# Layer 0 projection of a two-layer transformer: the bias rows in single-pass matmuls over 33 rows

## The reference, cut to what matters

```python
q = (layernorm(x, ln_q_g, ln_q_b) @ Wq + bq)            # 256 -> 256
kv = (layernorm(x, ln_kv_g, ln_kv_b) @ Wkv + bkv)       # 256 -> 512
q = apply_rotary(q * scale, x); k = apply_rotary(k * scale, x)
qn = layernorm(q, ln_h_g, ln_h_b); kn = layernorm(k, ln_h_g, ln_h_b)
```

## Time and profile before

| what | us |
|---|---|
| median of three runs | 2167.97 |
| the profiled execution, whole | 2167.56 |
| its span | 2165.9 |
| weights block, to the start of the next | 0 to 24.9 |
| projection block | 24.9 to 181 |
| PE busy in the span | 1929.3 (89%) |
| DVE busy in the span | 1472.4 (68%) |

### The profile page before, as it was taken

The page is one execution under the profiler, slowest core; times in us unless marked ns, Lnnn a source line. Parts: engine busy times, 40 slices in busy tenths (PEclk is TensorE's granted clock), DMA queues, the critical chain, the costliest instruction groups (busy, mean ns, idle before and its releaser), DMA issues. The chain is left out here.

```text
span 2165.9 us, 40750 instructions
## 1 busy us (share of the span) xinstructions
PE 1929.3 (89%) x11376; PEld 1297.2 (60%) x11438; DVE 1472.4 (68%) x3391; ACT 1222.2 (56%) x2508; POOL 896.3 (41%) x905
## 2 busy tenths in 40 slices
PE   4997999999959759999739899999998999999998
PEld 1452333333237659999725477777754777777787
DVE  4896888888548859999539576677365565653442
ACT  0683777777735237777314467767344777773331
POOL 1341000000027757798244187887300666662300
PEclk7895999999979979999969899999998999999999
DMA  7963000000072258899522011211101011111000
GB/s 205 289 145 59 2 0 0 1 0 1 1 203 96 98 172 265 265 282 279 178 66 61 4 47 42 57 45 49 35 1 39 24 25 35 25 35 39 11 10 20
DMA packets 185944, 173.87 MB, mean 80 GB/s; under 512 B 19651, under 2 KB 170741, under 8 KB 184822
## 3 DMA queue, kind: packets, MB, share of 16 engines
q1 hardware_dynamic: 173750, 143.23, 23.9%
q0 software_dynamic: 10720, 29.44, 4.1%
q10 hardware_dynamic: 1376, 0.02, 0.0%
HBM read 96.15 MB, written 61.60 MB: 73 GB/s over the span
## 5 line engine op out<-in xcount | busy, mean ns | idle before, releaser
L2633 POOL TENSOR_TENSOR w_rest<-work,w_head 128x512 fp32r<-128x512 f32 (+3 forms) x384 | 395.4, 1044 | 212.6 <-ACT w_head L2598 205.1
L767 DVE TENSOR_REDUCE half_max<-m_ps 128x1 f32<-128x512 f32 x512 | 317.4, 684 | 58.1 <-PE m_ps L689 57.7
L824 ACT ACTIVATE weights<-s_ps 128x512 f32<-128x512 f32 x512 | 266.2, 600 | 108.1 <-PE s_ps L707 108.1
L2594 ACT ACTIVATE work<-s_ps 128x512 f32<-128x512 f32 (+3 forms) x384 | 187.5, 488 | 113.2 <-PE s_ps L2423 91.1
L2598 ACT ACTIVATE w_head<-work 128x512 fp32r<-128x512 f32 (+3 forms) x384 | 201.4, 524 | 72.9 <-PE o_ps L2433 65.8
L689 PE MATMUL m_ps<-kT,qT 96*128 (+1 forms) x512 | 204.3, 400 | 8.4 <-DVE half_max L767 6.4
L707 PE MATMUL s_ps<-qT,kT 99*128 (+1 forms) x512 | 193.3, 384 | 9.5 <-DMA qT<-max_rows 5.1
L2433 PE MATMUL o_ps<-w_head,lat_head 128*128 128x512 f32 (+3 forms) x384 | 177.9, 463 | 7.1 <-POOL w_rest L2633 7.1
L864 POOL COPY v_now<-v 128x83 f32 (+1 forms) x64 | 16.0, 256 | 366.6 <-PE o_ps L719 361.7
L2474 DVE CUSTOM_DVE_ANT_0 work<-m_ps,mask_row 128x128 bf16<-128x128 f32 (+3 forms) x256 | 120.3, 485 | 49.2 <-PE m_ps L2391 46.2
L1072 POOL TENSOR_TENSOR gv_rest<-ex_wgv,gv_head 128x736 fp32r<-128x736 f32 x64 | 114.3, 1786 | 69.4 <-ACT gv_head L1169 69.4
(11 more groups left out here) (404 smaller groups left out, 5044.3 us busy)
## 6 DMA issues: line engine op xcount, KB each, us to landing
slots<-zero SPq DMA_DIRECT2D x8, 3456.0 KB, 27.5
rows<-slots SPq DMA_DIRECT2D x64, 256.0 KB, 3.4
slots<-ex_out SPq DMA_DIRECT2D x64, 256.0 KB, 3.0
ex_wgv<-in_L_ffn_wg_dram SPq DMA_DIRECT2D x72, 176.0 KB, 3.0
ex_wgv<-in_L_ffn_wv_dram SPq DMA_DIRECT2D x72, 176.0 KB, 3.3
ex_wo<-in_L_ffn_wo_dram SPq DMA_DIRECT2D x72, 128.0 KB, 3.2
oT<-work SPq DMA_DIRECT2D x64, 128.0 KB
w_down<-l_inverse SPq DMA_DIRECT2D x32, 256.0 KB, 3.9
```

The lines of the kernel that those rows point to most:

```text
L767: dve.tensor_reduce(half_max[:, u:u + 1], m_ps[:, BANK[u], :], AX.X, ALU.max).then_inc(max_done, 1)
L824: act.activation(w[:, s % 2 * 4 + j, :], s_ps[:, BANK[4 * s + j], :], ACT.Exp, scale=HD ** -0.5).then_inc(w_done, 1)
L2594: act.activation(w[:, s % 3, c0:512], s_ps[:, s % 3, c0:512], ACT.Exp, scale=SM1).then_inc(d["w_done"], 1)
L2633: pool.tensor_tensor(w_rest[:, s % 3, c0:512], w[:, s % 3, c0:512], w_head[:, s % 3, c0:512], ALU.subtract).then_inc(d["w_rest_done"], 1)
```

## The change

The bias row is split into a head, rounded to fp32r, and the remainder. Both stand in `bias_qkv`, now 33 partitions of fp32r: the head in row 0, the remainder in row 32, zeros between. The stationary operand is a block of ones of 33 partitions by 128 in fp32r. The bias matmul contracts 33 rows, once. POOL makes the zeros and ones in the weights block; the fp32 row of ones and its memset in `constants` go. DVE writes the sum to `bias_in`, copies it to row 0 and subtracts into row 32.

```diff
-        bias_qkv = l.sb("bias_qkv", [1, 3 * D])
+        bias_qkv = l.sb("bias_qkv", [BIAS_REST + 1, 3 * D], F32R)      # BIAS_REST = 32
+        ones = l.sb("bias_ones", [BIAS_REST + 1, P], F32R)
...
-            dve.memset(c.ones_row[:, :], 1.0)
...
-            dve.tensor_tensor(bias_qkv[0:1, 0:512], bias_ps[0:1, 0, :], bias_in[0:1, 0:512], ALU.add)
-            dve.tensor_tensor(bias_qkv[0:1, 512:768], bias_ps[0:1, 1, 0:256], bias_in[0:1, 512:768], ALU.add)
+            dve.tensor_tensor(bias_in[0:1, 0:512], bias_ps[0:1, 0, :], bias_in[0:1, 0:512], ALU.add).then_inc(summed, 1)
+            dve.tensor_tensor(bias_in[0:1, 512:768], bias_ps[0:1, 1, 0:256], bias_in[0:1, 512:768], ALU.add
+                              ).then_inc(summed, 1)
+            dve.wait_ge(summed, 2)
+            dve.wait_ge(blank, 4)
+            dve.tensor_copy(bias_qkv[0:1, :], bias_in[0:1, :]).then_inc(split, 1)
+            dve.wait_ge(split, 1)
+            dve.tensor_tensor(bias_qkv[BIAS_REST:BIAS_REST + 1, :], bias_in[0:1, :], bias_qkv[0:1, :], ALU.subtract)
+        @block.gpsimd
+        def _(pool):
+            pool.memset(plain[:, 0:3 * D], 0.0).then_inc(blank, 1)
+            pool.memset(plain[:, 3 * D:], 1.0).then_inc(blank, 1)
+            pool.wait_ge(blank, 2)
+            pool.tensor_copy(bias_qkv[:, :], plain[:, 0:3 * D]).then_inc(blank, 1)
+            pool.tensor_copy(ones[:, :], plain[:, 3 * D:]).then_inc(blank, 1)
...
-                        i = pe.matmul(qkv_ps[:, half, 0:w], c.ones_row[0:1, :],
-                                      bias_qkv[0:1, 512 * half:512 * half + w], start=False, stop=True)
+                        i = pe.matmul(qkv_ps[:, half, 0:w], ones[:, :],
+                                      bias_qkv[:, 512 * half:512 * half + w], start=False, stop=True)
```

More of the change, by code:

```diff
@@ L232, in __init__, with l0_weights @@
         self.mask_qk = m.sb("mask_qk", [P, P], BF16)
-        self.ones_row = m.sb("ones_row", [1, P])
         self.shift_rows = m.sb("shift_rows", [P, P], BF16)
-def l0_weights(block, nc, m, c, a, w_qkv, bias_qkv, g_h, b_h, rot):
+BIAS_REST = 32
+def l0_weights(block, nc, m, c, a, w_qkv, bias_qkv, ones, g_h, b_h, rot):
     with ExitStack() as ctx:
@@ L245, in l0_weights @@
         bias_in = l.sb("bias_in", [1, 3 * D])
+        plain = l.sb("bias_plain", [BIAS_REST + 1, 3 * D + P])
         bias_ps = l.ps("bias_ps", [P, 2, 512])
         loaded, scaled, biased = m.sem("w0_loaded"), m.sem("w0_scaled"), m.sem("w0_biased")
+        blank, summed, split = m.sem("w0_blank"), m.sem("w0_summed"), m.sem("w0_split")
         @block.sync
@@ L292, in _, with l0_project @@
             last.then_inc(biased, 1)
-def l0_project(nc, m, c, x, mean_var, rstd, norm_var, slots, zero, cleared, w_qkv, bias_qkv, g_h, b_h, rot, qT, kT, v, duplicated):
+def l0_project(nc, m, c, x, mean_var, rstd, norm_var, slots, zero, cleared, w_qkv, bias_qkv, ones, g_h, b_h, rot, qT, kT, v, duplicated):
     NH = 2 * H0
@@ L897, in layer0_attention @@
             layernorm_stats_in(block, Mem(nc, ctx2), m, "ln0", work, mean_var, rstd, loaded=loaded, again=norm_var)
-            l0_weights(block, nc, m, c, a, w_qkv, bias_qkv, g_h, b_h, rot)
+            l0_weights(block, nc, m, c, a, w_qkv, bias_qkv, ones, g_h, b_h, rot)
         qT = l.sb("qT", [P, B, H0, S], BF16)
@@ L902, in layer0_attention @@
         duplicated = m.sem("l0_duplicated")
-        l0_project(nc, m, c, work, mean_var, rstd, norm_var, slots, zero, cleared, w_qkv, bias_qkv, g_h, b_h, rot, qT, kT, v, duplicated)
+        l0_project(nc, m, c, work, mean_var, rstd, norm_var, slots, zero, cleared, w_qkv, bias_qkv, ones, g_h, b_h, rot, qT, kT, v, duplicated)
         att = work[:, :, :].rearrange("p t d -> p (t d)").rearrange("p (g q n) -> p g q n", g=NG, q=TB)
```

## The result

The changed kernel takes 2161.24 us (median of 20 runs, 2155.67 to 2165.39), the kernel before 2168.14 us (20 runs, 2162.30 to 2173.98). The ratio is 0.9967, with a 95% interval of 0.9959 to 0.9974: faster by 5.6 to 8.9 us, less than the 0.5% (10.8 us) that the prediction set as its line. The profiled execution took 2159.36 us (span 2157.8 us).

What follows compares the result with a forecast made beforehand. PE bounds the first, low-clock projections, DVE the full-clock steps. An earlier clock rise gains 10.8 us, the +1.6 us weights-block cost included: 2157.2 from the median, given as 2157.4 us, range 2153 to 2166.

Steps and rivals of the forecast that it cites:

- The bound: Projection: PE bounds at the low clock, DVE at full clock with 7.11 us a step, where faster bias matmuls gain 0.
- The bias matmul: Projection: 512 columns take 0.72 us instead of 2.00 at low clock; a projection saves 1.93 us, 0.96 at full clock.
- The weights block: Block's end: DVE's copy 0.6 us, subtraction 0.95, waits 0.1, together +1.6 us; POOL's work hidden, cost 0.
- The first projections: First projections: clock rises in the first or second, gain 10.8 us including the +1.6 us; chance 0.63.
- the "slower" rival: Full-clock steps: PE idles 1.2 us in each and the clock falls back; 2180 with every second step low; chance 0.05.
- the new spacing: First projections: spacing falls from 10.4 to 8.4 us, so the three barren attempts at a clock rise need not recur.
- the first of the three ends: Clock rises 4.1 us into the first projection, which ends at 42.1 us; fifth L392 at 68.7, gain 12.3 us.
- the late rise: Clock rises only in the third or fourth projection: gain 7.6 or 5.6 us, 2160 to 2162; rival's chance 0.19.
- Behind the projection: After the projection: all later blocks start behind a barrier and move as a whole.
- the signs of being wrong: Clock 0.50 past 60 us, a step under 6.9 us, 0.50 stretches between 71 and 150 us, or longer statistics.
- bound the full-clock steps: Rival, full-clock steps: PE rather than DVE sets the pace, 11.5 us more would go: 2146; chance 0.03.
- An early rise in both kernels: Rival, first projections: both kernels' clocks rise early, little gain against +1.6 us, about 2167; chance 0.10.

Runs made afterwards that it cites:

- the second execution: The changed kernel measured and profiled again, unaltered: 2160.91 us, ratio 0.9965 to the kernel before.
- the first profile: The first of three profiled executions of the unaltered changed kernel: span 2157.8 us; that kernel's median is 2161.24 us, ratio 0.9967.
- the split added: Kernel before plus the split's weights-block work, into buffers nobody reads, with its old bias matmul kept: 2172.54 us, ratio 1.0014.
- with warming: Seven extra matmuls ahead of the first transposes: on the kernel before 2167.15 us (0.9988), on that kernel with fp32 bias over 128 rows 2156.29 us (0.9935).
- the second measurement: Both kernels measured again, unaltered: changed kernel 2160.91 us, ratio 0.9965 (0.9954 to 0.9976).
- second execution of the kernel before: The kernel before measured and profiled again, unaltered: 2168.63 us, ratio 0.9998.

## Why the prediction was right, and where not

**The bound.** Right. In all 14 profiles DVE's step is 6.9 to 7.1 us at full clock whatever the bias matmul takes, and the new matmuls of these steps gained nothing: from the fifth reading to attention it is 101.2 us in the mean of three executions, before and after.

**The bias matmul.** Right: 0.73 us at the low clock (0.72 forecast), and 89.50 to 93.21, 3.71 us, for a projection at the full clock (3.7). The change of row count is a real cost: at the full clock 0.2 us go with equal row counts (0.86 us in place of 1.05). The 0.29 us of the low clock was not measured with equal ones.

**The weights block.** Right: 0.55 and 0.95 us, 1.56 us in all (1.6). POOL's work did not stretch the statistics (their aggregation began at 10.88 us in the second execution, at 10.81 to 10.90 in the three of the kernel before); the 0.3 us by which it was later in the first profile was a wait for x.

**The first projections.** That the gain is a clock that is up sooner was right; the size and the reason were not. I took 10.8 us, the middle between a rise in the first projection (12.3) and in the second (9.3), for 2157.4 us; three executions of each give 10.1 at the fifth reading, and the medians 6.9. Two things were taken as settled. First, from the rise on I let the clock stay up. In two of three profiles it fell again, at 54.2 us for 10.3 us (2.5 us lost) and at 51.8 us for 3.4. I had priced the idle time of the later steps, 1.2 us, and missed the gaps of the first ones, 1.49 us ahead of the third projection and 2.27 us in step 0, where no `turn_stack` is due; the "slower" rival was this mechanism, in the one place where it works, and at a tenth of its price. Second, the old kernel's one profile was its latest of three: 81.0 us, where the others had 77.4 and 80.7, so the base was 1.3 us too late.

**Why it was the clock, and not the spacing.** I explained an earlier rise by the new spacing of the projections. That is not what happened. In the first profile the clock rose ahead of the first new bias matmul, and the kernel before rose in its first projection too, once in three executions and again with the split added. So the early rise itself was in part luck of the execution. What the kernels do differ in is how long the clock then stays up, and the fp32 matmul over 128 rows has the long hold without the single pass (109 us in one execution; in the other, with warming, one fall of 3.4 us). Over the kernels this goes with the time in passes over few rows: 3.15 of 8.85 us at the low clock before, 1.2 of 6.9 after, none with 128 rows. That the kernel over one row in a single pass behaves like the changed one fits this.

**Readings and sums of the prediction.** It says that one-row matmuls fill the stretch from 37 to 40 us. They do not: PE is in the 128-row L567 until 38.64 us, and in the one-row L569 only after that. The 9.3 us without a pause shown above are the reading that its point needs. In the first of the three ends the terms give 42.4 and not 42.1 us for the end of the first projection, and in the last three projections and three rotations from 36.7 us end at 61.9 and not 62.7 us. The first moves the forecast by under 0.3 us; by the second the late rise would gain 6.4 us and not 5.6.

**Behind the projection.** I let the rest move as a whole. In the mean of three, from attention to the experts the changed kernel took 1.7 us less (one execution, with 596.2, makes most of it), and from layer 1 to the end both took the same. From the experts to layer 1 the old kernel took 355.8, 357.9 and 358.3 us, the changed one 360.4, 359.9 and 359.4: 2.6 us more in the mean. The clock is low in different places there, and other kernels show 356.3 to 360.3. Whether that is the change's doing or chance was not settled, nor was it tried. The three spans are 9.3 us apart in the mean, the medians 6.9 and, in the second measurement, 8.4: how much is lost behind the projection is known to a few microseconds only.

**The rivals.** A rise as late as before did not come in three executions (39.1, 40.6 and 48.4 us). Yet the measured 2161.24 us lies in that rival's 2160 to 2162 and not at the forecast's 2157.4: the time alone would have pointed to the wrong rival, and the traces tell them apart. Of the signs of being wrong two came by their letter. In the second execution the clock was at 0.50 past 60 us (54.2 to 64.5); it was a fall and not a late rise. In the first it fell at 148.3 us, ahead of 150, but behind the last projections, as the old kernel's did at 163.0. PE did not bound the full-clock steps. It waited 0.97 us in them where I expected about 1.2. An early rise in both kernels came once in three executions of the old one and did not last.

## What to carry to other kernels

A bias added by a one-row matmul can be dear in clock: here PE was busy without a pause for 9.3 us and granted 1.2 GHz. Before shortening such a matmul, widen it with zero rows to the row count of its neighbours; that alone gave here as much as the whole change (ratio 0.9950 against 0.9967, with intervals that meet), and it also saves the change of rows. And take three profiles of each kernel before you read a difference of 10 us in 2168: one pair showed 14 us at a place where the mean of three pairs shows 10.

## What the runs showed that I had not expected

- An fp32 matmul over 128 rows between others over 128 rows took 44.97 - 44.11 = 0.86 us for 512 columns at full clock; over one row it took 45.77 - 44.72 = 1.05 us (second execution of the kernel before). More rows are faster when the neighbours have them.
- Seven warming matmuls put the clock up and the old kernel lost it right behind its first projection: 34.1 us at the low level in a row with PE busy 30.4 of them.
- A window of PE with nothing but bf16 transposes took the clock from its low to its upper level (166.4 us, kernel before).
- In the first projections the clock fell in gaps of PE as short as 1.1 us (39.7 us, the kernel before with warming) and stayed up over gaps of 2.25 us (the changed kernel, first profile). Gaps alone do not say which.
